# A two-layer graph kernel with its first phase in a new order on every engine

## The reference

```python
# layer 0: attention of 8 heads over the edges of one destination
Q = (x[src] @ Wq + bq); K = (x[dst] @ Wk + bk); Vv = (x[dst] @ Wv + bv)
scores = einsum(Q, K per head) / sqrt(16) + (edge_attr @ Wb + bb)
alpha = softmax of scores over the edges with one dst
x1 = layernorm(x + (segment_sum(alpha * Vv, dst) @ Wo + bo))
# layer 1
h = x1 @ W
e = leaky_relu((h @ a1)[src] + (h @ a2)[dst], 0.2)
att = softmax(e)                       # over all edges
out = layernorm(x1 + segment_sum(att * h[src], dst))
```

## Time and profile before

| | us |
|---|---|
| median of three runs (lowest to highest) | 1305.71 (1303.69 to 1308.9) |
| the profiled execution | 1310.51 |
| its span | 1308.8 |
| busy in it: PE / DVE / ACT / POOL | 733.0 / 776.4 / 703.8 / 787.1 |

### The profile page before, as it was taken

How to read it: one execution, slowest core, us unless ns; L and a number is a source line. 1 busy time by engine, 2 the same in 40 slices (tenths; PEclk the granted TensorE clock), 3 DMA queues, 4 the chain that set the end, 5 groups by cost and what they waited for, 6 DMA issues and landing times.

```text
span 1308.8 us, 16204 instructions
## 1 busy us (share of the span) xinstructions
PE 733.0 (56%) x3263; PEld 501.9 (38%) x3263; DVE 776.4 (59%) x4008; ACT 703.8 (54%) x2047; POOL 787.1 (60%) x803
## 2 busy tenths in 40 slices
PE   2167767766766676677524555455456453453540
PEld 1045555545544454555524445455452111111110
DVE  2367667776766776678734555555527565464651
ACT  0257767767777687688512333333355454354542
POOL 7677666666766676660036665566643666556665
PEclk9577787778778877877756776777767666666775
DMA  5246556565465655656143767767643222222210
GB/s 138 67 124 209 179 182 198 168 226 176 155 215 181 195 172 179 206 164 234 65 147 119 215 214 213 213 210 221 209 138 121 63 79 71 69 66 71 76 47 26
DMA packets 81840, 196.96 MB, mean 150 GB/s; under 512 B 19746, under 2 KB 21815, under 8 KB 81732
## 3 DMA queue, kind: packets, MB, share of 16 engines
q1 hardware_dynamic: 56558, 148.29, 35.2%
q0 software_dynamic: 25184, 47.65, 12.4%
HBM read 122.71 MB, written 77.22 MB: 153 GB/s over the span
## 4 chain that ended last, share of the span: by engine, by line
ACT 36%; another core or an unknown queue 28%; issue 17%; DVE 12%; PE 6%; POOL 1%; ACTq 0%; POOLq 0%; DVEq 0%
ACT h_res L642 9%; ACT node_out L642 8%; ACT yb L642 7%; DVE node_out L1152 3%; PE psum L599 3%; DVE part L1158 2%; DVE nst L1164 2%; ACT h_res L693 2%; ACT xsT L764 2%; ACT h_res L664 2%; ACT h_res L745 1%; PE psum L606 1%; ACT h_res L651 1%; ACT xsT L740 1%
## 5 line engine op out<-in xcount | busy, mean ns | idle before, releaser
L442 POOL DMA_INDIRECT out_dram<-yb,at_last x196 | 195.0, 995 | 134.6 <-ACT yb L642 75.3
L438 POOL DMA_INDIRECT xs<-in_x,src_tab x196 | 187.1, 955 | 126.1 <-remote 76.0
L438 POOL DMA_INDIRECT xs<-x_all,row_tab x196 | 187.4, 956 | 111.4 <-remote 56.4
L438 POOL DMA_INDIRECT h_res<-in_x,dst_tab x196 | 212.4, 1084 | 59.7 <-issue 59.7
L532 PE MATMUL psum<-xsT,h_res 128*128 128x512 f32 x98 | 93.2, 1051 | 155.0 <-ACT h_res L693 155.0
L627 PE MATMUL psum<-node_out,ident_inv 128*128 128x512 f32 x98 | 80.8, 919 | 149.1 <-DVE node_out L1152 105.3
L642 ACT ACTIVATE h_res<-node_in,shift,rstd 128x128 f32<-128x128 f32 (+1 forms) x392 | 155.8, 486 | 6.3 <-DVE shift L907 3.6
L599 PE MATMUL psum<-w,xsT 128*128 128x129 f32 x392 | 85.5, 386 | 110.3 <-ACT xsT L740 109.7
L740 ACT ACTIVATE xsT<-psum 128x512 f32<-128x512 f32 x49 | 29.3, 597 | 206.6 <-remote 125.5
L599 PEld LDWEIGHTS psum<-w,xsT 128*128 128x128 f32 x392 | 75.8, 287 | 118.5 <-ACT xsT L740 116.7
L642 ACT ACTIVATE yb<-psum,shift,rstd 128x128 f32<-128x128 f32 x196 | 73.8, 457 | 67.4 <-remote 33.5
(11 more groups left out here) (253 smaller groups left out, 1988.5 us busy)
## 6 DMA issues: line engine op xcount, KB each, us to landing
x1d_in<-x_all SPq DMA_DIRECT2D x98, 256.0 KB
node_in<-in_x SPq DMA_DIRECT2D x48, 512.0 KB
x_all<-h_res SPq DMA_DIRECT2D x48, 512.0 KB
out_dram<-node_out SPq DMA_DIRECT2D x48, 512.0 KB
x_all<-yb SPq DMA_DIRECT2D x49, 256.0 KB
src_b<-src_t SPq DMA_DIRECT2D x49, 256.0 KB
node_in<-x_all SPq DMA_DIRECT2D x24, 512.0 KB
h_res<-in_edge_attr SPq DMA_DIRECT2D x7, 784.0 KB
```

Source lines behind the costliest of these rows:

```text
L438: return pool.indirect_dma_start(out=to, out_offset=None, in_=table, in_offset=bass.IndirectOffsetOnAxis(ap=idx, axis=0))
L442: return pool.indirect_dma_start(out=table, out_offset=bass.IndirectOffsetOnAxis(ap=idx, axis=0), in_=rows, in_offset=None, bounds_check=l ...
```

## The change

- *Phase 1, order.* PE's step is now turn_dst(s), outputs(s-2), turn_src(s), keys and queries(s), values(s), turn_weighted(s-1), scores(s). A group passes in four steps: y at s+2, layernorm at s+3. `xT_done` is split into `xd_T` and `xs_T`; POOL's reuse of the source ring waits for `xs_T` alone. DVE and ACT have new orders that go with it; the ring `XDT` of turned destination rows goes from 4 to 2.
- *Nodes run ahead.* Node chunks run five steps (`AHEAD`) before the edge groups of the same number: three steps with nodes only come first, and the last three edge steps have none. Scaling for the output goes in halves of a chunk. Even chunks but the first are the late ones.
- *Drain.* The seven draining steps are gone; the last groups' items stand one by one between those of the fix-up.
- *Wide variances.* In phase 1, five operations on all twelve tiles' statistics at once (`spread`) take the place of twelve BN_AGGR a step.
- *Phase 2.* `LEAD` is 3: the row lookup of group s+3 stands in step s. Late chunks are scaled in halves, one each step.
- *Between.* The logits of the first 48 groups are made before the last group's rows are kept; the running sums begin before the softmax's sum is there.
- *Phase 3.* ACT weighs two groups ahead, between the scale and the apply of group s; a group needs two steps. The number of matmuls, of gathers and of scatters is unchanged.

```diff
-    LEAD = 6
-    DRAIN = 7
-    XS, XD, XDT, YB, NI, NX, NO, SB, XI = 4, 8, 4, 4, 3, 3, 2, 7, 4
+    LEAD = 3
+    AHEAD = 5
+    FIRST = 2 - AHEAD
+    XS, XD, XDT, YB, NI, NX, NO, SB, XI = 4, 8, 2, 4, 3, 3, 2, 7, 4
...
-        return k % 2 == 1
+        return k > 0 and k % 2 == 0
...
-                wait(pool, xT_done, g - XS + 1)
+                wait(pool, xs_T, g - XS + 1)
...
+            for s in range(GROUPS):
+                turn_dst(s)
+                if edge(s - 2):
+                    outputs(s - 2)
+                turn_src(s)
+                keys_and_queries(s)
+                values(s)
...
+                if edge(s - 1):
+                    turn_weighted(s - 1)
+                scores(s)
...
+            for s in range(FIRST, GROUPS):
...
+                if edge(s):
+                    copy_dst(s)
+                if edge(s - 1):
+                    weights(s - 1)
+                if s - 3 >= -AHEAD:
+                    deviations(s - 3)
+                if edge(s):
+                    copy_src(s)
+                out_half(s - 4 + AHEAD - 1, 1)
+                out_half(s - 4 + AHEAD, 0)
+                if edge(s):
+                    queries(s)
+                if edge(s - 3):
+                    apply_rows(s - 3)
...
+                if edge(s - 1):
+                    copy_weighted(s - 1)
+                if edge(s - 3 + AHEAD):
+                    apply_nodes(s - 3 + AHEAD)
...
+                if s + LEAD < GROUPS:
+                    rows_of(s + LEAD)
...
+            weigh(0)
+            weigh(1)
+            for s in range(GROUPS):
...
+                if edge(s + 2):
+                    weigh(s + 2)
```

More of the change, by code:

```diff
@@ L495, in rows_of, with outputs @@
+            def outputs(g):
+                pe.wait_ge(hv_turned, g + 1)
+                wait(pe, y_done, g)
+                if g == 0:
+                    pe.wait_ge(prep_act, 3)
+                add_bias(bank[6], 1)
+                for t in range(G):
+                    last = mm(tile(bank[6], t), tile(hT[:, g % 2, :], t), wo[:, :], start=False, stop=t == G - 1)
+                last.then_inc(o_mm, 1)
             def rows_of(r):
@@ L737, in _ @@
+            for s in range(GROUPS + 1):
+                g = s - 1
                 if edge(s):
```

1139 lines of the change are left out of this document (600 added, 539 removed).

## The result

The changed kernel took 1348.34 us, median of four runs (1343.86 to 1349.63), beside 1305.01 us of the kernel before: a ratio of 1.0321, with a 95% interval from 1.0288 to 1.0354. It is slower by 43 us, and outside the stated range by 3.

A forecast was written before the change was run, and what follows sets the result against it. The prediction took POOL's cycle of indirect DMA streams, stops and held signals as the steady bound. Terms 0 + 0 − 6 − 22 + 15 − 5 − 4 − 4 = −26 gave 1280 us, range 1243 to 1345.

The forecast's parts named there:

- The view that signals are held: All phases: a PE or DVE signal raised late in an unbroken POOL stream reaches other engines only after the stream.
- the first rival: Phase 1, shorter steps: POOL's credit comes before signals are held, step 11.3 us, −29, total 1251 us; chance 0.15.
- Steady steps of phase 1: Some 41 steps: credit raised about as deep in POOL's stream, so 12.0 us stays, 0; best case −29.
- The second rival: Phase 1: held hv_T delays source transposes; step 14.2 us, +90, 1370 us; every second step caught, +41, 1321; chance 0.24.
- Start: Three node-only steps come first, POOL's stream of forty gathers stays the same: 0, from −10 to +8.
- Drain: Last source copy to first gather of x1: last groups pass in fewer steps, −22, from −30 to −10.
- last steps: End of phase 1: the last three steps lose a node apply of 3.18 us, −6, from −9 to 0.
- Phase 2: Lookup three groups ahead makes POOL's gathers wait for it: +15, from 0 to +38.
- Between the phases: Before phase 3: running sums start earlier, logits are split, a group needs two steps: −5, from −8 to 0.
- Phase 3: POOL's scatter cycle: weighing two groups ahead shortens or lengthens its stops, −4, from −20 to +12.
- Tail: After the last group of phase 3, one step is lost: −4.
- The rule of the most-contended engine: Whole kernel: make the busiest engine, POOL, faster first; a reorder leaving its 784 issues alone gains 0, 1306 us.

The follow-up runs named there:

- held_after: Changed kernel, three POOL memsets behind each group's gathers; ACT's copy of weighted rows and DVE's use of scores wait for later groups' memsets: 1309.96 us.
- held_swap: As held_after, but PE's turn_weighted stands ahead of values and the wait of ACT's copy of weighted rows is left out: 1185.72 us.
- weightop: Changed kernel with phase 3's weighing on ACT put ahead of the wait for the group's variance: 1067.38 us.
- the pauses: Three chained POOL memsets between each group's source and destination gathers: kernel before from 1129.17 to 1212.81 us, changed kernel from 1066.4 to 1151.30.
- swap: Changed kernel with PE's turn_weighted(s-1) put ahead of values(s) in phase 1: 1068.42 us.
- lead6: Changed kernel with the row lookup six groups ahead instead of three: 1073.50 us.

## Why the prediction was wrong

The forecast was 26 us less; measured were 39 more by the spans. The 65 us between them are some 30 in the steady steps of phase 1, 12 at the start, 16 in phase 3 and 6 in the tail, with small amounts elsewhere.

*The view that signals are held* fits the traces of its session, before and after. Its form was too strict. I wrote that a late signal "reaches the others only after the stream"; the changed kernel's hv_T came ahead of the stream's end in half of the steps. And it is a condition of that session and not of the program, as the unchanged programs show. The sign that the last sentence of the prediction names, something else that holds the signals, is thus half seen: the stream alone does not hold them. One figure has no row: the 1.41 us for each indirect DMA, from which the 11.3 us of the first rival come. The two divisions shown give 1.45 and 1.47, and the streams themselves took 10.4 us before and 9.8 after.

*Steady steps of phase 1* is the step that failed: "so the credit is raised about as deep in the stream. I take 12.0 us, no change: **0**". Measured +0.7 us a step, some 30 us over 41: +1.28 in POOL's stops and −0.58 in its gathers. The argument followed POOL's credit alone and passed over what stands ahead of it on PE: outputs(s−2), which waits for a copy, which waits for hv_T, raised 6.2 us into the stream in the short step shown and 7.2 in the long one. The second rival had this chain; held_after shows that a late hv_T is enough to lengthen the step, and held_swap fits that. The rival's price for a caught step was near (14.2 us against 13.6), partly by luck: in most of them the signal came 0.2 to 0.3 us after the stream's end and not 1.5 as it said, while PE at the lower clock took longer. Half of the steps were caught, its milder case, with +41. The −0.58 was not in the prediction at all. I had called POOL's gathers the same.

*Start*, 0 from −10 to +8: the kernel is one step behind, some 12 us, since the source copy of group 0 is queued behind a node's logs on ACT, which waited 26.07 us for DVE, and so misses the time ahead of 61 us. I had called the stream of forty gathers the same; it is, but who gets through ahead of its end is not.

*Drain*, −22: from the last copy to the first gather of x1 I had named 32 us instead of 53.7:

```profile
683.43 1.02 POOL L477 DMA_INDIRECT x_all<-x1f,carry_idx  x1 [54.68 <-issue]
686.44 0.97 POOL L473 DMA_INDIRECT xs<-x_all,row_tab  x1 [1.99 <-DVE row_tab L1004]
```

It is 686.44 − 658.7 = 27.7, so −26.0. The *last steps*, which I had put at −6, took 24.8 us instead of 28.1 by the starts of the copies, −3.3. Together −29.3 where I had −28: this part was right, and it holds in both sessions.

*Phase 2*, +15: measured +15.7. POOL now waits 72.2 us for row_tab in place of 56.4 us on "remote", and ten of its 30 stops are 3.7 to 4.1 us, the 4 that was named for them. In the session without holding the lead of three costs nothing (0.7 us less than before). So the size and the place agree with the argument; that +15 was hit so closely is luck, since it was a choice between 0, 21 and 38. No run gives the lookup its lead back under holding.

*Between the phases*, −5: −3.2. *Phase 3*, −4: +12.2, the upper end of its bounds. The weighing stands in a loop of ACT and DVE, which weightop opens (4.12 us instead of 5.0), and which I had costed only in POOL's restart. Without holding phase 3 costs 2.4 us, since four scatters at 1.29 us are 5.16 us a group and cover a pace of 5.0. *Tail*, −4: +2.1.

*The rule of the most-contended engine* (the Trainium skill, "Perfetto Trace Analysis", "Identifying the Most-Contended Engine") names POOL in the kernel before when nothing is held, with 70% of the span busy against DVE's 68%, and rightly: POOL's issue sets the time, the pauses add to it one for one, and what took 32 us off POOL's gathers took 31 us off the kernel. In the changed kernel it names DVE (75% against POOL's 72%), though there too the pauses add one for one; POOL's 0.30 us between two gathers are not counted as busy. I had said that the change leaves POOL's issues alone; it leaves their number alone. In the first session the rule explains nothing, since POOL had less work and more time went by.

What stays open: why the first session held the signals of PE and DVE and the later ones did not. The profile has one word for it, "remote". Round trips beside POOL's gathers alone did not bring it out, and no session of 1305 us came back. So nothing was changed while signals were held: the chain is read from the traces there and imitated elsewhere, and no run shows whether swap, lead6 and weightop help there.

## What to carry to other kernels

Before an item is put ahead of the one that renews the slowest queue's credit, ask what that item waits for, and through how many engines; put the transposes, or whatever raises the credit, ahead of anything that needs a round trip. Two orders that take the same time when all signals are prompt (1066.4 and 1068.4 us) need not have the same slack: with one signal made late by hand the first took 1310 us, and the second, in which that signal is raised earlier and was left alone, 1186. Before a gain is put down to a new order, undo the small edits that came with it one by one: here one operand gave 33 of the 34 us of phase 1 by itself. An operand moved from SBUF to PSUM on DVE can speed up POOL, and the time of the POOL rows beside it tells.

## What the runs showed of the hardware

- The same program took 1305 us in one session and 1129 us in others, with the same duration of ACT's copy (597 ns) and 12 us more work on PE; the rest of the difference is waits, which in the first session end on "remote" and in the others never do.
- A DVE addition of two SBUF operands (1.22 us) makes a gather that starts on POOL during it take 1.18 to 2.09 us instead of 0.94 (47 of 48), and with the second operand in PSUM it does not (0 of 48).
- A round trip from PE to ACT and back (one 128x128 transpose, one copy) took 0.84 us, also beside 40 gathers on POOL.
- The same eight output matmuls took 1.05 us at a granted clock of 1.00 and 1.91 us at 0.50, within 13 us of one trace.
